# Maxima stage and convolution: thirty-two more row sums on ScalarE, features written in place, gates by a sigmoid

## The reference, cut to what matters

```python
B, C, L = x.shape                     # 16, 64, 2048; x is the layer norm of the input here
k = _crucial_k(C)                     # 38
_, topk_idx = jax.lax.top_k(moveaxis(channel_map, 1, 2), k)   # over 1601 channels
mask = zeros((B, L, C)).at[b_idx, l_idx, topk_idx].set(1.0)
crucial_features    = mask * x        # mask with the channel axis moved back
subcrucial_features = (1 - mask) * x
c_max = max(crucial_features, axis=1);     c_avg = mean(crucial_features, axis=1) * (C / k)
s_max = max(subcrucial_features, axis=1);  s_avg = mean(subcrucial_features, axis=1) * (C / (C - k))
# conv1d over L, 2 channels in, 1 out, 7 taps, padding 3; then with mean and variance over B and L:
A = sigmoid(relu((z - mu) * rsqrt(var + 1e-5) * gamma + beta))    # A_S1 of crucial, A_S2 of subcrucial
out = crucial_features * A_S1 + subcrucial_features * A_S2
```

## Time and profile before

| | |
|---|---|
| median of 3 runs | 2354.77 us (2352.66 to 2357.07) |
| the profiled execution | 2347.9 us, span 2346.1 us |
| PE, PEld busy | 85%, 70% of the span |
| DVE, ACT, POOL busy | 61%, 43%, 40% |
| stats stage | from 801.4 us, when L822 first starts, to 863.6 us, when L815 last ends |
| conv stage | from there to 891.6 us |
| mean granted TensorE clock | 0.953 |

### The profile page before, as it was taken

The page is one execution under the profiler, slowest core; times in us unless marked ns, Lnnn a source line. Parts: engine busy times, 40 slices in busy tenths (PEclk is TensorE's granted clock), DMA queues, the critical chain, the costliest instruction groups (busy, mean ns, idle before and its releaser), DMA issues. The chain is left out here.

```text
span 2346.1 us, 39096 instructions
## 1 busy us (share of the span) xinstructions
PE 1996.5 (85%) x15210; PEld 1633.0 (70%) x15210; DVE 1431.2 (61%) x2343; ACT 1008.6 (43%) x2006; POOL 930.0 (40%) x855
## 2 busy tenths in 40 slices
PE   4777788788882054899999999999999999999999
PEld 4666566667762044688787888887778888878887
DVE  6999899999998898764444550134445524731111
ACT  6777767677771036432322332222333422522221
POOL 1221111112220150466554555555555535644554
PEclk9999899899996577999999999999999999999999
DMA  9999787789980203452225444322235436434443
GB/s 366 373 363 325 271 281 264 249 313 326 321 300 15 85 1 99 157 153 80 75 82 172 138 140 125 99 82 81 77 128 162 152 103 209 138 112 130 141 143 120
DMA packets 150088, 407.69 MB, mean 174 GB/s; under 512 B 15376, under 2 KB 36112, under 8 KB 148112
## 3 DMA queue, kind: packets, MB, share of 16 engines
q1 hardware_dynamic: 149616, 403.55, 50.7%
q0 software_dynamic: 288, 1.64, 0.2%
HBM read 379.96 MB, written 25.17 MB: 173 GB/s over the span
## 5 line engine op out<-in xcount | busy, mean ns | idle before, releaser
L1158 POOL TENSOR_TENSOR t<-t,t 128x512 fp32r<-128x512 f32 (+1 forms) x488 | 651.1, 1345 | 676.7 <-ACT t L1151 676.3
L1704 PE MATMUL ps<-t,t 128*128 128x512 f32 x1856 | 739.7, 399 | 19.7 <-POOL t L1158 9.4
L1706 PE MATMUL ps<-t,t 128*128 128x512 f32 x1856 | 725.4, 391 | 0.0
L1705 PE MATMUL ps<-t,t 128*128 128x512 f32 x1856 | 724.9, 391 | 0.0
L1151 ACT ACTIVATE t<-t 128x512 fp32r<-128x512 f32 (+1 forms) x488 | 295.5, 608 | 704.5 <-PE ps L1706 384.1
L704 PE MATMUL ps<-t,t 128*128 128x128 bf16 (+1 forms) x6656 | 454.0, 224 | 165.7 <-DVE t L442 155.1
L704 PEld LDWEIGHTS ps<-t,t 128*128 128x128 bf16 x6656 | 403.3, 101 | 266.7 <-DVE t L442 216.5
L442 DVE TENSOR_SCALAR t<-t,t 128x1601 bf16<-128x1601 f32 x512 | 515.7, 1050 | 3.6 <-DVE t L615 0.4
L665 ACT ACTIVATE t<-t,t 128x1601 bf16<-128x1601 f32 x256 | 416.5, 1627 | 79.4 <-DVE t L598 77.3
L1704 PEld LDWEIGHTS ps<-t,t 128*128 128x128 f32 x1856 | 349.3, 188 | 100.5 <-POOL t L1158 14.0
L1706 PEld LDWEIGHTS ps<-t,t 128*128 128x128 f32 x1856 | 349.2, 188 | 74.1
(11 more groups left out here) (214 smaller groups left out, 1698.9 us busy)
## 6 DMA issues: line engine op xcount, KB each, us to landing
t<-ctxT SPq DMA_DIRECT2D x256, 800.5 KB, 5.9
t<-wqkv SPq DMA_DIRECT2D x192, 256.0 KB, 3.2
t<-wo SPq DMA_DIRECT2D x128, 256.0 KB, 4.6
t<-wb SPq DMA_DIRECT2D x128, 256.0 KB, 3.3
t<-xT SPq DMA_DIRECT2D x32, 256.0 KB, 6.6
t<-xT SPq DMA_DIRECT2D x2, 4096.0 KB, 12.1
t<-x1d SPq DMA_DIRECT2D x32, 256.0 KB, 4.9
x2d<-t SPq DMA_DIRECT2D x32, 256.0 KB, 2.0
```

What stands on the lines that cost most here:

```text
L1158: e.tensor_tensor(wlo[r][:, 0:nk, :], raw[r][:, 0:nk, :], wh[r][:, 0:nk, :].bitcast(F32), ALU.subtract).then_inc(w_lo, 1)
L1704: e.matmul(bank[:, :], wh[r][:, q, :], xl, start=(kt == 0), stop=False)
L1705: e.matmul(bank[:, :], wlo[r][:, q, :], xh, start=False, stop=False)
L1706: m = e.matmul(bank[:, :], wh[r][:, q, :], xh, start=False, stop=(c == NCH[p] - 1 and q == nk - 1))
```

## The change

ScalarE sums six batches (8 to 13) instead of four, and VectorE only the last two. VectorE writes the two maxima straight into `Yp` (`feature[0]`, `feature[1]`), and so does the scaling of the two sum features; one of these two and the copy of the sums out of `ps[5]` move to ScalarE. The edge matmuls read `Yp`, ScalarE copies their results in, and VectorE begins with the centre tap (3), which needs no edge; taps 0, 1, 2 wait for the left edge, 4, 5, 6 for the right. Some steps lose their wait, the variance and its epsilon are made in one operation. Scale, shift and clamp become two Relu activations with the scale and shift from per-partition operands, and the exponential, the addition and the reciprocal become two Sigmoid activations, the second of which writes `A2` directly. `in_turn`'s counted step numbers (`CV`) go, and semaphores of their own take their place.

```diff
-    BY_ACT, BY_DVE = range(8, 12), range(12, 16)
+    BY_ACT, BY_DVE = range(8, 14), range(14, 16)
+    feature = [Yp[:, B * f:B * f + B, 3:19] for f in range(4)]
+    row_sums = stat[:, 2, :, :]
 def stats_vector(e):
-            e.tensor_reduce(stat[:, 1, b, :], sbc[b % 2][:, :, :], AX.X, ALU.max).then_inc(rest_max, 1)
+            e.tensor_reduce(feature[1][:, b, :], sbc[b % 2][:, :, :], AX.X, ALU.max).then_inc(rest_max, 1)
-            e.tensor_reduce(stat[:, 0, b, :], crc_of(b), AX.X, ALU.max)
+            e.tensor_reduce(feature[0][:, b, :], crc_of(b), AX.X, ALU.max).then_inc(top_max, 1)
         for b in range(B - LAG, B):
-            total(b)
+            if b in BY_DVE:
+                total(b)
             rest(b)
 def stats_scalar(e):
+            if b == BY_ACT[-2]:
+                e.wait_ge(sums8, 1)
+                e.activation(row_sums[:, 0:HB, :], ps[5][...], ACT.Copy).then_inc(sums_out, 1)
 def conv_vector(e):
-        do(e.tensor_copy(stat[:, 2, 0:HB, :], ps[5][...]))
-        do(e.tensor_tensor(stat[:, 3, :, :], ps[6][...], stat[:, 2, :, :], ALU.subtract))
-        do(e.tensor_scalar(stat[:, 2, :, :], stat[:, 2, :, :], 1.0 / C, C / K, ALU.mult, ALU.mult))
-        do(e.tensor_scalar(stat[:, 3, :, :], stat[:, 3, :, :], 1.0 / C, C / (C - K), ALU.mult, ALU.mult))
-        do(e.tensor_copy(Yp[:, :, 3:19], st))
-        e.wait_ge(conv_edges, 1)
-        do(e.tensor_copy(Yp[:, :, 0:3], edge[0]))
-        e.wait_ge(conv_edges, 2)
-        do(e.tensor_copy(Yp[:, :, 19:22], edge[1]))
+        sums_there(e)      # all row sums of ScalarE and VectorE, and the copy from ps[5]
+        do(e.tensor_tensor(stat[:, 3, :, :], ps[6][...], row_sums, ALU.subtract))
+        e.tensor_scalar(feature[3], stat[:, 3, :, :], PART[1], None, ALU.mult).then_inc(f_in, 1)
+        e.wait_ge(rest_max, B)
+        e.wait_ge(top_max, B)
+        e.wait_ge(f_in, 2)
+        for n, tap in enumerate([3, 0, 1, 2, 4, 5, 6]):
+            if n in (1, 4):
+                e.wait_ge(f_edge, 1 + n // 4)
+            for ch in range(2): ...
         for s in range(2):
-            do(e.tensor_scalar(Z[:, s, :], Z[:, s, :], sc[:, s:s + 1], None, ALU.subtract))
+            e.tensor_scalar(Z[:, s, :], Z[:, s, :], sc[:, s:s + 1], None, ALU.subtract).then_inc(z_centred, 1)
-        do(e.tensor_scalar(sc[:, 4:6], PA[1][:, 0:2], 1.0 / (B * L), None, ALU.mult))
-        do(e.tensor_scalar(sc[:, 8:10], sc[:, 4:6], EPS, None, ALU.add))
+        e.tensor_scalar(sc[:, 8:10], PA[1][:, 0:2], 1.0 / (B * L), EPS, ALU.mult, ALU.add).then_inc(z_var, 1)
         do(e.reciprocal(sc[:, 12:14], sc[:, 10:12]))
-        for s in range(2):
-            do(e.tensor_scalar(Z[:, s, :], Z[:, s, :], sc[:, 12 + s:13 + s], w16[:, 14:15], ALU.mult, ALU.mult))
-        do(e.tensor_scalar(Z[:, :, :], Z[:, :, :], w16[:, 15:16], 0.0, ALU.add, ALU.max))
-        e.wait_ge(z_exp, 1)
-        do(e.tensor_scalar(Zt[:, :, :], Zt[:, :, :], 1.0, None, ALU.add))
-        do(e.reciprocal(A12[:, :, :], Zt[:, :, :]))
-        do(e.tensor_tensor(Dm, A12[:, 0, :]..., A12[:, 1, :]..., ALU.subtract))
-        e.tensor_copy(A2, A12[:, 1, :]...).then_inc(gates, 1)
+        e.tensor_scalar(sc[:, 14:16], sc[:, 12:14], w16[:, 14:15], None, ALU.mult).then_inc(z_scale, 1)
+        e.wait_ge(z_out, 4)
+        e.tensor_tensor(Dm, A1[:, :, :], A2, ALU.subtract).then_inc(gates, 1)
 def conv_scalar(e):
+        sums_there(e)
+        e.activation(feature[2], row_sums, ACT.Copy, scale=PART[0]).then_inc(f_in, 1)
+        for x_, cols in ((0, slice(0, 3)), (1, slice(19, 22))):
+            e.wait_ge(conv_edges, x_ + 1)
+            e.activation(Yp[:, :, cols], edge[x_], ACT.Copy).then_inc(f_edge, 1)
         e.activation(sc[:, 10:12], sc[:, 8:10], ACT.Sqrt).then_inc(z_std, 1)
-        e.activation(Zt[:, :, :], Z[:, :, :], ACT.Exp, scale=-1.0).then_inc(z_exp, 1)
+        e.wait_ge(z_scale, 1)
+        for s in range(2):
+            e.activation(Zt[:, s, :], Z[:, s, :], ACT.Relu, scale=sc[:, 14 + s:15 + s], bias=w16[:, 15:16]).then_inc(z_out, 1)
+        for s in range(2):
+            e.wait_ge(z_out, s + 1)
+            e.activation((A1[:, :, :], A2)[s], Zt[:, s, :]..., ACT.Sigmoid).then_inc(z_out, 1)
```

More of the change, by code:

```diff
@@ L320, in build @@
     Zt = at(162 * KB, [2, 256])
-    A12 = at(164 * KB, [2, 256])
+    A1 = at(164 * KB, [B, NT])
     Zg = at(qr_off, [544])
@@ L796, in build @@
     crucial, rest_set, rest_max = sem("crucial"), sem("rest_set"), sem("rest_max")
-    crucial_sum, sums8, v_sums = sem("crucial_sum"), sem("sums8"), sem("v_sums")
+    crucial_sum, sums8, v_sums, top_max = sem("crucial_sum"), sem("sums8"), sem("v_sums"), sem("top_max")
     LAG = 4
-    BY_ACT, BY_DVE = range(8, 12), range(12, 16)
+    BY_ACT, BY_DVE = range(8, 14), range(14, 16)
+    sums_out = sem("sums_out")
+    feature = [Yp[:, B * f:B * f + B, 3:19] for f in range(4)]
+    row_sums = stat[:, 2, :, :]
     def xn_of(b):
@@ L814, in rest @@
             e.wait_ge(rest_set, b + 1)
-            e.tensor_reduce(stat[:, 1, b, :], sbc[b % 2][:, :, :], AX.X, ALU.max).then_inc(rest_max, 1)
+            e.tensor_reduce(feature[1][:, b, :], sbc[b % 2][:, :, :], AX.X, ALU.max).then_inc(rest_max, 1)
         def total(b):
-            e.tensor_reduce(stat[:, 2, b, :], crc_of(b), AX.X, ALU.add).then_inc(v_sums, 1)
+            e.tensor_reduce(row_sums[:, b, :], crc_of(b), AX.X, ALU.add).then_inc(v_sums, 1)
         e.wait_ge(opened, 1)
@@ L852, in stats_scalar, with sums_there @@
                 e.activation(jnk[:, :], crc_of(b)[:, t, :], ACT.Copy,
-                             accum_out=stat[:, 2, b, t:t + 1]).then_inc(crucial_sum, 1)
+                             accum_out=row_sums[:, b, t:t + 1]).then_inc(crucial_sum, 1)
                 n += 1
-    turn_conv = sem("turn_conv")
-    conv_edges, z_total, z_std, z_exp, gates = (sem("conv_edges"), sem("z_total"), sem("z_std"), sem("z_exp"), sem("gates"))
-    st = stat[:, :, :, :].rearrange("p f b t -> p (f b) t")
-    edge = [PA[1][:, 0:192].rearrange("p (g t) -> p g t", t=3), PA[2][:, 0:192].rearrange("p (g t) -> p g t", t=3)]
-    CV = {"padded": 5, "sum": 22, "sqsum": 27, "var": 29, "relu": 33}
+            if b == BY_ACT[-2]:
+                e.wait_ge(sums8, 1)
+                e.activation(row_sums[:, 0:HB, :], ps[5][:, 0:HB * NT].rearrange("p (b t) -> p b t", t=NT),
+                             ACT.Copy).then_inc(sums_out, 1)
+    turn_conv, z_part = sem("turn_conv"), sem("z_part")
+    f_in, f_edge, conv_edges, z_total = sem("f_in"), sem("f_edge"), sem("conv_edges"), sem("z_total")
+    z_centred, z_sums, z_var, z_std, z_scale, z_out, gates = (sem("z_centred"), sem("z_sums"), sem("z_var"), sem("z_std"),
+                                                              sem("z_scale"), sem("z_out"), sem("gates"))
+    edge = [PA[1][:, 0:192].rearrange("p (g t) -> p g t", t=3), PA[2][:, 0:192].rearrange("p (g t) -> p g t", t=3)]
+    PART = [float(np.float32(C / K)) / C, float(np.float32(C / (C - K))) / C]
+    TAPS = [3, 0, 1, 2, 4, 5, 6]
+    def sums_there(e):
+        e.wait_ge(crucial_sum, NT * len(BY_ACT))
+        e.wait_ge(v_sums, len(BY_DVE))
+        e.wait_ge(sums_out, 1)
     def conv_vector(e):
@@ L866, in conv_vector @@
         e.wait_ge(xn_sum, 32)
-        e.wait_ge(crucial_sum, NT * len(BY_ACT))
-        e.wait_ge(v_sums, len(BY_DVE))
+        sums_there(e)
+        do(e.tensor_tensor(stat[:, 3, :, :], ps[6][:, 0:256].rearrange("p (b t) -> p b t", t=NT), row_sums, ALU.subtract))
+        e.tensor_scalar(feature[3], stat[:, 3, :, :], PART[1], None, ALU.mult).then_inc(f_in, 1)
         e.wait_ge(rest_max, B)
[L870 to L873, removed]
-        do(e.tensor_scalar(stat[:, 2, :, :], stat[:, 2, :, :], 1.0 / C, C / K, ALU.mult, ALU.mult))
-        do(e.tensor_scalar(stat[:, 3, :, :], stat[:, 3, :, :], 1.0 / C, C / (C - K), ALU.mult, ALU.mult))
-        do(e.tensor_copy(Yp[:, :, 3:19], st))
-        e.wait_ge(conv_edges, 1)
-        do(e.tensor_copy(Yp[:, :, 0:3], edge[0]))
-        e.wait_ge(conv_edges, 2)
-        do(e.tensor_copy(Yp[:, :, 19:22], edge[1]))
+        e.wait_ge(top_max, B)
+        e.wait_ge(f_in, 2)
         Zf = Z[:, :, :].rearrange("p s (b t) -> p (s b) t", t=NT)
-        for ch in range(2):
-            for tap in range(7):
+        for n, tap in enumerate(TAPS):
+            if n in (1, 4):
+                e.wait_ge(f_edge, 1 + n // 4)
+            for ch in range(2):
                 src = Yp[:, ch * 32:ch * 32 + 32, tap:tap + 16]
                 wsc = w16[:, ch * 7 + tap:ch * 7 + tap + 1]
-                if ch == 0 and tap == 0:
+                if ch == 0 and n == 0:
                     do(e.tensor_scalar(Zf, src, wsc, None, ALU.mult))
@@ L889, in conv_vector @@
                     do(e.scalar_tensor_tensor(Zf, src, wsc, Zf, ALU.mult, ALU.add))
-        do(e.tensor_reduce(sc[:, 2:4], Z[:, :, :], AX.X, ALU.add))
+        e.tensor_reduce(sc[:, 2:4], Z[:, :, :], AX.X, ALU.add).then_inc(z_part, 1)
         e.wait_ge(z_total, 1)
```

(34 more changed lines are left out.)

1 line of the change is left out of this document (added).

## The result

| | before | changed |
|---|---|---|
| median | 2352.66 us (6 runs, 2351.99 to 2357.07) | 2345.35 us (6 runs, 2343.63 to 2346.76) |
| ratio | | 0.997, 95% interval 0.996 to 0.998 |
| profiled execution: span | 2346.1 us | 2342.4 us |
| first mask product of stats (S) | 801.39 us | 804.63 us |
| `gates` | S + 90.21 | S + 83.69 |

The kernel became 7.3 us faster. The spans alone differ by 3.7 only, because the profiled execution of the changed kernel reached S 3.2 us later, before any changed instruction. That part and the part after `gates` scatter by a few microseconds from one execution to the next (S from 801.4 to 805.7 and `gates` to the end from 1453.7 to 1459.5 us over the profiles of this study, in no order that follows the edits). `gates` is read at the start of VectorE's first operation behind it.

A forecast was written before the change was run, and what follows sets the result against it. A single serial thread in conv, ending at `gates`, was taken to bound the kernel. Savings 2.38 + 0.12 + 0.20 + 2.86 = 5.56 us against 2354.8 gave 2349.2 us; own range 2347.8 to 2352, with rivals 2345.8 to 2353.2.

The forecast's parts named there:

- five signs: Prediction wrong if row sum over 0.384, load before Relus, pause behind load, Sigmoid dearer than Exp, first product losing lead.
- the 0.47: Gate: time from the end of ScalarE's two-column square root to VectorE's reciprocal, taken over unchanged as 0.47 us.
- the hidden load: Rival at the gate: the table load follows the square root and costs 0.42 instead of 1.31; 0.9 more gain, chance 0.10.
- the edge stall: Features and edges: VectorE waits 0.25 us for the left edge after the two centre taps; range nothing to 0.5.
- the copy's 0.31: End of stats: ScalarE's copy out of PSUM among its 96 row sums, 0.28 us, with its gap 0.31.
- Stats: End of the row sums: ScalarE with 96 rows becomes last, so the subtraction starts 0.63 us later.
- Features and edges: From the subtraction to the reduce before the mean: the stage is 2.38 us ahead there, the 0.63 included.
- Mean and variance: One wait fewer saves 0.12 us; variance and epsilon in one operation save 0.20.
- The gate: End of the square root to `gates`: 4.60 us instead of 7.46, so 2.86 us saved.
- That rival: After `gates`: weight waits or TensorE's clock take back part of the gain, giving 2352 to 2355 us; chance 0.17.
- a slower pace of the row sums: Rival in stats: ScalarE's 96 rows end to end at 0.45 us each cost 6.3 us more; chance 0.04.
- a pause behind the load: Rival at the gate: dead time of 1.3 us at the table switch; gain 4.3, 2350.5 us; chance 0.07.

The follow-up runs named there:

- experiment 1: Kernel before with only the split of row sums changed: ScalarE sums batches 8 to 13, VectorE 14 and 15; 2354.06 us, ratio 1.0003.
- experiment 6: Changed kernel with row sums split as before, four batches on ScalarE and four on VectorE; 2343.72 us, ratio 0.9962.
- experiment 7: Changed kernel with the taps in their old order, 0 to 6, so the first waits for the left edge; 2348.43 us, ratio 0.9977.
- experiment 3: Changed kernel with scale, shift and clamp back on VectorE in three operations, the two Sigmoid left on ScalarE; 2345.36 us, ratio 0.9965.
- experiment 9: Changed kernel with two Exp for the two Sigmoid, and addition, reciprocal and copy back on VectorE; 2350.53 us, ratio 0.9989.
- Experiments 2 and 5: Kernel before with one unread ScalarE Copy, behind the Sqrt (2: 2353.3 us) or after the reduce before the mean (5: 2349.73 us).
- 10 and 11: Kernel before with eight VectorE memsets ahead of stats (10: 2351.7 us) or 32 ScalarE copies ahead of its row sums (11: 2352.88 us).

## Why the prediction was wrong

**Which way and how far.** The direction was right and the chain was the one described; the time fell 0.45 us below the range, and the gain of 7.3 us is more than the 5.6 forecast. The 3.9 us between 2349.2 and 2345.35 are three parts: 2.1 from the level, 1.0 from the sum, 0.8 that the chain does not show. None of the five signs by which the prediction said that it would be wrong came: a row sum still took 0.384, the load stood behind the Relus with 0.01 us to the first Sigmoid, a Sigmoid cost what an Exp costs, and the first product kept the lead. What failed are sizes, and with the largest of them, the 0.47, also the reading of what it is the price of.

**The level.** "The sum stands against the median" put the 5.56 us against 2354.8, the median of three runs; six runs gave 2352.66, which is the 2.1. How much of it is the fault of the level stays open: the 63 later runs of the kernel before have medians of 2353.87, 2353.49 and 2354.54, so 2354.8 was 0.2 to 1.3 too high by them and the six runs were low. By them the part that nothing explains is larger, 1.6 to 2.7 us.

**The range.** It gave two microseconds to the scatter of medians, the hidden load its 0.9, and bounds to the Sigmoids, the row sums and the edge stall. Its low end before the hidden load, 2347.8, does not follow from the terms named for it: 0.4 and 0.25 less than 2349.2 are 2348.6. No term that turned out wrong had a bound in it: not the 0.47 to VectorE, not the copy's 0.31, not TensorE's two calls.

**The steps of the sum that failed: 0.96 us short (5.56 against 6.52), 0.43 of it in "0.47 to VectorE".** Position by position:

| from S to | forecast | measured | off by |
|---|---|---|---|
| subtraction after the sums | 63.43 | 63.10 | 0.33 |
| the reduce before the mean | 75.20 | 74.87 | 0.33 |
| end of the Sqrt | 80.05 | 79.57 | 0.48 |
| `gates` | 84.65 | 83.69 | 0.96 |

The line of the kernel before at the first of its two calls to TensorE, for the third point below:

```profile
880.40 0.16 DVE L892 TENSOR_SCALAR t<-ps 128x2 f32<-128x2 f32 x1 [0.75 <-PE ps L917]
```

- *Stats.* ScalarE became last, as forecast, and at 0.384 a row. The copy out of PSUM, which I had at 0.31, cost nothing: the row sums ahead of it and behind it started at 861.14 and 861.58, 0.44 apart, as the change of batch one before, which has no copy, shows them (855.00 and 855.44). That (0.31) and a shorter way to VectorE (0.09 instead of 0.11) are the 0.33. Calling this part a cost was right: 0.6 (experiment 1), 0.96 within the changed kernel (experiment 6).
- *Features and edges.* Right to 0.01 from the subtraction to the reduce; the order of the taps is worth 1.3 of it (experiment 7).
- *Mean and variance.* Two calls to TensorE cost 0.07 less each: VectorE's idle time before the mean's scaling is 0.68 in the changed kernel and was 0.75, and it is so in every profile of the two families of kernels. By the code what differs there is `do`'s wait ahead of the wait for the result, which is gone; no run changes that alone. I had counted the waits that went between VectorE's own steps and not these: 0.15.
- *The gate.* 4.12 us instead of 4.60. The Relus (1.09 against 1.08), the bare load (1.29 against 1.31) and the Sigmoids (0.72 against 0.76) were right; experiment 3 shows that the load costs what it lies bare, and experiment 9 that a Sigmoid costs what an Exp costs. Of the 0.48, 0.43 is the single step "0.47 to VectorE", which took 0.04. I read the 0.47 as what a short Sqrt costs, and it was not its price. Experiments 2 and 5 exclude ScalarE's next instruction and its idle time, 10 and 11 tie 0.37 of it to the place in VectorE's program; the other 0.06 is, by the code, again a wait of `do` (0.10 in experiments 1 and 10, which have it, 0.03 to 0.04 in the changed kernel and its variants, which have not). What is left, 0.05, is a balance: the 128x2 scaling took 0.23 and not 0.17, the way from the last Sigmoid to VectorE 0.04 and not 0.11, and the Sigmoids 0.04 less.

**The rest, 7.3 in the medians against 6.5 on the chain,** lies inside the interval (4.7 to 9.4 us). The stages after `gates` kept the lead: the products began 6.5 us earlier and the profiled execution ended 6.9 earlier, counted from S. TensorE's clock began alike too: its mean granted clock in the first three stretches of 10 us behind `gates` was 0.50, 0.84 and 0.84 in both kernels, where 0.50 is the lower level, 1.2 GHz, and 1.00 the upper, 2.4 GHz. Further on it was lower in the changed kernel in some stretches (0.67 against 0.80 from 40 to 50 us behind `gates`), and the lead of 6.26 us stood behind them. That rival fell for this pair of profiles, and so did the hidden load (the load stands behind the Relus), a slower pace of the row sums and a pause behind the load.

## What to carry to other kernels

On a serial chain across engines, sum it row by row: here each stage came out right to half a microsecond. Then look at which engine ends each stage last, because handing work to an idle engine can make that engine the last one (six batches lose 0.96 us against four, five win 0.63). A table load cost here only what nothing covered: keep a step of another engine between the function that evicts a table and the one that needs the next. A gap between two engines that is read at one place may belong to that place: give it a bound. And set the forecast against a level that is as uncertain as the runs are.

## What was not expected of the hardware

- VectorE shows a pause of 0.2 to 0.4 us that stands at a place of its program and not at an operation: 0.37 us ahead of the reciprocal in four kernels with the same VectorE program, gone from there in each of the others, and (in one profile) 0.21 us ahead of another instruction when eight were put in front. What happens at that place was not looked into; its cause stays open.
- A 128x128 copy of 0.26 us between the row sums of two batches on ScalarE took none of its time: it fitted into the 0.44 us that the step from one batch to the next takes anyway.
- The fifth mask product of stats took 2.35 to 2.90 us where its neighbours took 1.22, in every profile. Its cause stays open.
